# Linear attention, softmax attention and routed experts on 8 cores: token buffer cleared during attention, sums inverted by GpSimd, and the output stage and the end reordered

## The reference

```
xn = layernorm(x)
# recurrent layer, 8 heads of 128
q, k, v = xn Wq^T, xn Wk^T, xn Wv^T
s = (rmsnorm(causal_linear_attention(q, k, v) / denom)) Wo^T
# attention and experts
h1   = rmsnorm(xn) * g1
q    = h1 Wq ;  c = h1 Wdkv ;  k, v = c Wuk, c Wuv        # 16 heads of 64
att  = softmax(causal(q k^T / 8)) v
h2   = xn + att Wo
t    = rmsnorm(h2) * g2
top2 = top_k(t gate_w, 2) ; gates = softmax(top2)           # 8 experts
moe  = sum over the 2 chosen experts e of gate_e * silu(t w1_e) w2_e     # w1: 1024x2048
g    = silu(h2 + moe)
y    = x + s * g
```

## Time and profile before

| what | value |
|---|---|
| time, median of 3 runs | 1753.93 us (1749.98 to 1757.81) |
| the profiled execution | 1748.96 us, its span 1747.4 us |
| spans of the 8 cores | 1722.2 to 1747.4 us, slowest core 6 |
| TensorE matmul busy | 1384.2 us, 79% |
| TensorE weight load busy | 616.0 us, 35% |
| VectorE busy | 724.8 us, 41% |
| ScalarE busy | 583.4 us, 33% |
| GpSimd busy | 387.1 us, 22% |
| moved by DMA | 225.31 MB, mean 129 GB/s |

### The profile page before, as it was taken

How to read it: one execution, slowest core, us unless ns; L and a number is a source line. 1 busy time by engine, 2 the same in 40 slices (tenths; PEclk the granted TensorE clock), 3 DMA queues, 4 the chain that set the end, 5 groups by cost and what they waited for, 6 DMA issues and landing times.

```text
span 1747.4 us, 24421 instructions; the slowest of 8 cores (1722.2 to 1747.4 us)
## 1 busy us (share of the span) xinstructions
PE 1384.2 (79%) x7553; PEld 616.0 (35%) x7665; DVE 724.8 (41%) x1205; ACT 583.4 (33%) x736; POOL 387.1 (22%) x457
## 2 busy tenths in 40 slices
PE   0758899999867788888467319999999999995456
PEld 0324445544312222222133204554555554542122
DVE  2347766548556654433536511212221222123255
ACT  1112222212346688999223202222222222222011
POOL 4212322248442211111103420000000000036410
PEclk9979999999958898999789759999999999998678
DMA  9734435400194000000198679996999997746899
GB/s 203 152 81 114 76 60 96 78 22 1 31 237 154 1 1 1 1 1 1 30 211 216 171 152 186 181 195 127 189 203 185 191 193 142 153 152 211 249 256 253
DMA packets 143427, 225.31 MB, mean 129 GB/s; under 512 B 74160, under 2 KB 81712, under 8 KB 143280
## 3 DMA queue, kind: packets, MB, share of 16 engines
q0 software_dynamic: 51568, 132.91, 39.5%
q1 hardware_dynamic: 91712, 90.43, 19.6%
HBM read 227.14 MB, written 62.45 MB: 166 GB/s over the span
## 4 chain that ended last, share of the span: by engine, by line
PE 57%; DMA 11%; DVE 11%; issue 8%; SPq 6%; ACT 4%; POOL 2%; DVEq 0%; another core or an unknown queue 0%; ACTq 0%; POOLq 0%; PEldq 0%
PE ps L1405 13%; PE pA L1373 7%; PE pB L1373 6%; PE pA L211 4%; PE pA L261 4%; DMA p4a<-ybuf,rcpos 4%; PE ps L790 4%; SPq L1539 3%; ACT ap L805 3%; PE pA L754 3%; PE pB L754 2%; PE pA L215 2%; DMA oxn<-x 2%; PE pw L790 2%; DVE ap L825 2%
## 5 line engine op out<-in xcount | busy, mean ns | idle before, releaser
L1405 PE MATMUL ps<-p3w,mhT 128*128 128x512 bf16 x1116 | 254.3, 381 | 3.8 <-issue 1.9
L805 ACT ACTIVATE ap<-pA,p2nmub 128x1024 bf16<-128x1024 f32 (+1 forms) x160 | 176.2, 1102 | 61.4 <-PE pA L754 56.3
L1528 DVE TENSOR_SCALAR my<-ps,mgate 128x512 f32<-128x512 f32 x78 | 58.3, 750 | 314.2 <-PE ps L1405 311.2
L211 PE MATMUL pA<-fxT,fw 128*128 128x512 bf16 x492 | 127.8, 413 | 67.4 <-DMA fxT<-fxb 41.8
L1405 PEld LDWEIGHTS ps<-p3w,mhT 128*128 128x128 bf16 x1152 | 111.6, 98 | 130.7 <-issue 4.3
L790 PE MATMUL ps<-ap,p2vaug 128*68 128x512 bf16 (+1 forms) x320 | 123.2, 385 | 39.6 <-DVE ap L825 38.5
L805 ACT ACTIVATE ap<-pB,p2nmub 128x1024 bf16<-128x1024 f32 (+3 forms) x160 | 142.2, 889 | 22.6 <-PE pB L754 22.3
L1489 ACT ACTIVATE mh<-pA 128x512 bf16<-128x512 f32 x78 | 46.2, 597 | 307.7 <-PE pA L1373 296.3
L1373 PE MATMUL pA<-p3w,mxT 128*128 128x512 bf16 x576 | 132.7, 384 | 4.7 <-issue 4.7
L1373 PE MATMUL pB<-p3w,mxT 128*128 128x512 bf16 x557 | 126.2, 379 | 1.2 <-issue 0.2
L211 PEld LDWEIGHTS pA<-fxT,fw 128*128 128x128 bf16 x512 | 51.3, 104 | 132.4 <-issue 88.7
(11 more groups left out here) (235 smaller groups left out, 2229.4 us busy)
## 6 DMA issues: line engine op xcount, KB each, us to landing
p3w<-w POOLq DMA_DIRECT2D x16, 4096.0 KB, 37.7
ybuf<-my SPq DMA_DIRECT2D x36, 512.0 KB, 8.0
ybuf<-zero POOLq DMA_DIRECT2D x1, 11776.0 KB, 71.4
mx<-hbuf SPq DMA_DIRECT2D x36, 257.5 KB, 8.2
fx<-x SPq DMA_DIRECT2D x16, 512.0 KB, 5.3
oxn<-x SPq DMA_DIRECT2D x16, 512.0 KB
...
```

The lines of the kernel that those rows point to most:

```text
L211: m = t.matmul(bank, wv[:, n // 8, k, 128 * m0:128 * (m0 + 1)], xv[:, k, :], start=(k == 0), stop=(k == DK - 1))
L805: a.activation(dst[:, :, 0:w], src[:, :, 0:w], AF.Exp, bias=c.p2nmub[:, p % 8:p % 8 + 1]).then_inc(c.a_exp, 1)
L1405: m = t.matmul(c.ps(4 + sl), c.mhT[:, 128 * k:128 * (k + 1)], c.p3w2[:, o:o + 512], start=(k == 0), stop=(k == 15))
L1528: v.tensor_scalar_mul(c.my[n % 2][:, sl * 512:(sl + 1) * 512], c.ps(4 + sl), c.mgate[n % 2][:, :]).then_inc(c.m_yev, 1)
```

## The change

1. *The inverses.* `invert` and its calls leave VectorE. In `att_gpsimd`, POOL raises the four sums to the power of -1 (a constant `minus`, broadcast over 4x1024) straight into the bf16 buffer `arl`, behind the last sum of every fourth unit. TensorE waits for one such instruction a group instead of two.
2. *Clearing.* `clear_results` also clears all of `hbuf`, eight DMAs of 17 x 128 rows from POOL. The eight DMAs at the end of routing, their table `tabzero` and its two VectorE instructions go. POOL waits for the clearing ahead of its first scatter instead of SP ahead of its first load.
3. *o2.* A new `att_sync` on SP turns the 16 tiles of o2 during attention, through one buffer `turn`, into a second DRAM buffer `o2T_sp`; `p4_sync` loads from it without a transpose.
4. *Output stage.* Four buffers `oxn` that lie in the half of `p3w1` that the second expert's weight takes later; SP loads them behind the last product of attention, before the outputs are scaled. TensorE waits for the gate weights only where it uses them first. `ossq` has two buffers. `oh3b` has twelve tiles and scatters go tile by tile from i = 8 on. The first weight comes in four DMAs of 1 MB as written, at i = 2, 5, 8 and 11.
5. *Experts and end.* The four loads of h2 go from POOL to SP, at the start of the last expert, found by a new table `tablast`. SP no longer waits for the results of unused slots. The first expert's first product is issued without a branch. `p4_vector` waits for the lower sum tile by tile instead of for all 16.

The diff, cut:

```diff
 
-    def invert(g):
-
-        l, rl = c.al[g % 2], c.arl[g % 2]
-        v.wait_ge(c.a_ladd, 8 * (g + 1))
-        v.reciprocal(l[64:68, :], l[64:68, :]).then_inc(c.a_rl, 1)
-        v.wait_ge(c.a_rl, 2 * g + 1)
-        if g >= 2:
-            v.wait_ge(c.a_bc, 8 * (g - 1))
-        v.tensor_copy(rl[64:68, :], l[64:68, :]).then_inc(c.a_rl, 1)
...
@@ -842,18 +833,13 @@
             scale(p - 8)
         mask(p, 2)
         mask(p, 3)
-        if p >= 4 and p % 4 == 0:
-            invert(p // 4 - 1)
         v.wait_ge(c.a_pv, FIRST[p + 1])
         if blk:
             v.wait_ge(c.a_ladd, 2 * (p - 7))
         for o, bank in zip((c.aoa, c.aob), o_banks(c, p)):
             v.tensor_copy(o[0:68, 512 * m:512 * (m + 1)],
                           bank[0:68, 0:512]).then_inc(c.a_ev, 1)
-    for p in range(NPAIR - 8, NPAIR - 4):
-        scale(p)
-    invert(7)
-    for p in range(NPAIR - 4, NPAIR):
...
         [128, 2 * (NSLOT - 16), DM // 2])).then_inc(c.y_clear, 16)
+    tokens = c.D["hbuf"].ap().rearrange("(e p r d) -> e p r d", p=128, r=REGION // 128, d=ROW * 2)
+    for e in range(NEXP):
+        g.dma_start(tokens[e], c.zero[:, :].bitcast(U8).unsqueeze(1).broadcast_to(
+            [128, REGION // 128, ROW * 2])).then_inc(c.z_out, 16)
+
+
+def att_sync(s, c):
+
+    for q in range(2):
+        s.wait_ge(c.f_o2out[q], 16 * 8)
+    for i in range(NTI):
+        if i:
+            s.wait_ge(c.t_out, 16 * i)
+        s.dma_start_transpose(c.turn[:, :].rearrange("p (k t) -> p k t", t=128),
+                              tok(c.D["o2_sp"], i)).then_inc(c.t_in, 16)
+        s.wait_ge(c.t_in, 16 * (i + 1))
+        s.dma_start(tok(c.D["o2T_sp"], i), c.turn[:, :]).then_inc(c.t_out, 16)
+    s.wait_ge(c.t_out, 16 * NTI)
 
...
+        if m % 4 == 3:
+            n = p // 4
+            g.wait_ge(c.a_ladd, 2 * (p + 1))
+            if n >= 2:
+                g.wait_ge(c.a_bc, 8 * (n - 1))
+            g.tensor_tensor(c.arl[n % 2][64:68, :], l[64:68, :],
+                            c.minus[64:68, 0:1].broadcast_to([4, 1024]), OP.pow).then_inc(c.a_rl, 1)
...
-TD = 14
+OXN = 4
...
 def o_sync(s, c):
-    s.wait_ge(c.a_mul, 2 * NPAIR)
-    for i in range(NTI + 1):
-        if i < NTI:
-            if i >= 2:
-                s.wait_ge(c.o_h2, 2 * (i - 1))
-            s.dma_start(c.oxn[i % 2][:, :], tok(c.D["x"], i)).then_inc(c.o_xnr[i % 2], 16)
-        if i >= 1:
-            s.wait_ge(c.o_h2, 2 * i)
-            s.dma_start(tok(c.D["h2_sp"], i - 1),
-                        c.oh2[(i - 1) % 3][:, :]).then_inc(c.o_h2out[(i - 1) % 3], 16)
+    s.wait_ge(c.a_pv, len(STEPS))
+    for i in range(OXN):
+        load_rest_x(s, c, i)
+    for i in range(NTI):
+        s.wait_ge(c.o_h2, 2 * (i + 1))
+        s.dma_start(tok(c.D["h2_sp"], i), c.oh2[i % 3][:, :]).then_inc(c.o_h2out[i % 3], 16)
+        if i + OXN < NTI:
+            load_rest_x(s, c, i + OXN)
...
+
+def load_rest_x(s, c, i):
+    s.dma_start(c.oxn[i % OXN][:, :], tok(c.D["x"], i)).then_inc(c.o_xnr[i % OXN], 16)
...
-    t.wait_ge(c.o_gld, 16)
     for i in range(NTI + 4):
...
+            if j == 0:
+                t.wait_ge(c.o_gld, 16)
...
-            if j >= 8:
-                v.wait_ge(c.o_scat[2 * (j % 4)], 16 * (j // 4 - 1))
-                v.wait_ge(c.o_scat[2 * (j % 4) + 1], 16 * (j // 4 - 1))
-            v.scalar_tensor_tensor(c.oh3b[:, ROW * (j % 8):ROW * (j % 8) + DM], c.oh2[j % 3][:, :], c.or3[:, j:j + 1],
+            if j >= 12:
+                v.wait_ge(c.o_scat[2 * (j % 4)], 16)
+                v.wait_ge(c.o_scat[2 * (j % 4) + 1], 16)
+            v.scalar_tensor_tensor(c.oh3b[:, ROW * (j % 12):ROW * (j % 12) + DM], c.oh2[j % 3][:, :], c.or3[:, j:j + 1],
                                    c.g2b[:, :], OP.mult, OP.mult).then_inc(c.o_h3, 1)
...
-
-    v.tensor_tensor(c.rzero[:, :], c.ps(5, 0, 8), c.rcon[:, 32:40], OP.add).then_inc(c.r_zero, 1)
-    v.wait_ge(c.r_zero, 1)
-    v.tensor_scalar_mul(c.tabzero[:, :], c.rzero[:, :], 2.0 * ROW).then_inc(c.r_zero, 1)
...
-    load_w1(g, c, 0)
-    for i in range(NTI + 5):
+    for i in range(NTI + 8):
...
-        if i >= 8 and i % 4 == 0:
-            b = (i - 8) // 4
-            g.wait_ge(c.r_pos, 2 * (b + 1))
-            for q in range(4):
-                j = 4 * b + q
-                g.wait_ge(c.o_h3, j + 1)
-                for k in range(2):
-                    if b:
-                        g.wait_ge(c.o_scat[2 * q + k], 16 * b)
-                    g.indirect_dma_start(
-                        hb, bass.IndirectOffsetOnAxis(c.rpos[:, 16 * k + j:16 * k + j + 1], 0),
-                        c.oh3b[:, ROW * (j % 8):ROW * (j % 8 + 1)].bitcast(U8), None).then_inc(c.o_scat[2 * q + k], 16)
+        if i in (2, 5, 8, 11):
+            load_first_w1(g, c, i // 3)
+        if i == 8:
+            g.wait_ge(c.z_out, 16 * NEXP)
+        if i >= 8:
+            scatter(g, c, hb, i - 8)
+
+
+def scatter(g, c, hb, j):
+
+    g.wait_ge(c.r_pos, 2 * (j // 4 + 1))
+    g.wait_ge(c.o_h3, j + 1)
+    for k in range(2):
+        s = c.o_scat[2 * (j % 4) + k]
+        if j >= 4:
+            g.wait_ge(s, 16 * (j // 4))
+        g.indirect_dma_start(
+            hb, bass.IndirectOffsetOnAxis(c.rpos[:, 16 * k + j:16 * k + j + 1], 0),
+            c.oh3b[:, ROW * (j % 12):ROW * (j % 12 + 1)].bitcast(U8), None).then_inc(s, 16)
+
+
+def load_first_w1(g, c, q):
+
+    g.dma_start(c.p3w1[:, 2 * q * EXPD:2 * (q + 1) * EXPD].rearrange("p (k n) -> p k n", n=EXPD),
+                rows3(c.D["w1_0"])[:, 2 * q:2 * (q + 1), :]).then_inc(c.w1ld[0], 16)
 
 
...
     g.wait_ge(c.ydone, NEXP - 1)
     g.wait_ge(c.r_fin, 10)
     for i in range(NTI + 1):
         if i < NTI:
             if i >= 2:
                 g.wait_ge(c.p4_low, i - 1)
-            if i % 4 == 0:
-                part = c.p4hh[i // 8][:, 4096 * (i // 4 % 2):4096 * (i // 4 % 2 + 1)]
-                g.dma_start(part.rearrange("p (i n) -> p i n", n=DM),
-                            h2[:, i:i + 4, :]).then_inc(c.p4_hld[i // 4], 16)
             gather_result(g, c, c.p4a[i % 2], i, c.p4_ald[i % 2])
         j = i - 1
         if j >= 0:
...
-        load(n)
-    s.wait_ge(c.y_clear, 16)
-    for n in range(NSLOT):
-        if n + MXN < NSLOT:
...
-        s.wait_ge(c.m_yev, 2 * (n + 1))
-        if n < SURE:
-            store(n)
-        else:
...
+    def load_rest():
+
+        h2 = c.D["h2_sp"].ap().rearrange("(i p) n -> p i n", p=128)
+        for q in range(4):
+            s.dma_start(c.p4hh[q // 2][:, 4096 * (q % 2):4096 * (q % 2 + 1)].rearrange(
+                "p (i n) -> p i n", n=DM), h2[:, 4 * q:4 * q + 4, :]).then_inc(c.p4_hld[q], 16)
+
...
+                    if n + 1 >= NEXP - 1:
+                        with s.register(f"rest{n}") as q:
+                            s.reg_load(q, c.tablast[0:1, n + 1:n + 2])
+                            with s.If_ne(q, 0):
+                                load_rest()
...
+        with s.register(f"out{n}") as r:
+            s.reg_load(r, c.tabval[0:1, n:n + 1])
+            with s.If_ne(r, 0):
+                s.wait_ge(c.m_yev, 2 * (n + 1))
+                store(n)
+                hand_on(n)
+            with s.Else():
+                s.wait_ge(c.m_yst[n % 2], 16 * (n // 2))
+                s.sem_inc(c.m_yst[n % 2], 16)
...
-    new_w1(0)
-    up(0, 0)
-    up(0, 1)
+
+    t.wait_ge(c.w1new, 1)
+    t.sem_inc(c.w1new, -1)
+    t.wait_ge(c.m_xev, 1)
+    up_with(0, 0, 0)
+    up_with(0, 1, 0)
...
+        s.dma_start(c.p4o[q][:, :], tok(c.D["o2T_sp"], i)).then_inc(c.p4_in[q], 16)
         s.dma_start(c.p4x[q][:, :], tok(c.D["x"], i)).then_inc(c.p4_in[q], 16)
 
...
 def p4_vector(v, c):
-    v.wait_ge(c.p4_low, NTI)
     for i in range(NTI + 1):
         if i < NTI:
...
-        ("tabnew", 40, I32, 0), ("tabval", 40, I32, 0), ("tabodd", 40, I32, 0), ("tabzero", 8, I32, 0), ("rzero", 8, F32, 0)])
-    region(route, [("oxn", DM, F32, 2), ("oh2", DM, F32, 3), ("oh3b", 8 * ROW, BF16, 0),
+        ("tabnew", 40, I32, 0), ("tabval", 40, I32, 0), ("tabodd", 40, I32, 0)])
+    c.tablast = c.rcmp[:, 0:40].bitcast(I32)
+    region(w1_end - DK * EXPD * 2, [("oxn", DM, F32, OXN)])
+    region(route, [("oh2", DM, F32, 3), ("oh3b", 12 * ROW, BF16, 0),
```

More of the change, by code:

```diff
@@ L852, in att_vector @@
                           bank[0:68, 0:512]).then_inc(c.a_ev, 1)
-    for p in range(NPAIR - 8, NPAIR - 4):
-        scale(p)
-    invert(7)
-    for p in range(NPAIR - 4, NPAIR):
+    for p in range(NPAIR - 8, NPAIR):
         scale(p)
@@ L1268, in p3_sync @@
     hb = c.D["hbuf"].ap()
-    s.wait_ge(c.z_set, 1)
-    s.wait_ge(c.r_zero, 2)
-    for e in range(NEXP):
-        with s.register(f"zero{e}") as r:
-            s.reg_load(r, c.tabzero[0:1, e:e + 1])
-            row = s.snap(r, donate=True, min_val=0, max_val=(HROWS - 128) * ROW * 2)
-            s.dma_start(hb[bass.ds(row, 128 * ROW * 2)].rearrange("(p n) -> p n", p=128),
-                        c.zero[:, :].bitcast(U8)).then_inc(c.z_out, 16)
-    s.wait_ge(c.r_tab, 18)
```

(48 more changed lines are left out.)

47 lines of the change are left out of this document (26 added, 21 removed).

## The result

| | before | changed |
|---|---|---|
| time, median | 1755.87 us (4 runs) | 2997.0 us (2990.56 to 2999.36, 4 runs) |
| ratio to before | | 1.708, 95% interval 1.702 to 1.714 |
| profiled execution, span | 1747.4 us (core 6) | 2993.2 us (core 1) |

The account below looks back on a forecast made before the run. No engine fills the span, so the chain of waits, read by stage, was taken as the bound. Terms -2 -5 -12 -5 -27 -15 -13 = -79 from 1749, plus 5, gave 1675 us, range 1620 to 1755.

Parts of the forecast that it names:

- point 1: Attention: inverses as powers on POOL, 7 us each; gains of 2 us in the middle and 5 us at the end.
- Rival A: Attention: each power is slow, 157 us along the line of short powers; time about 2870 us, chance 0.19.
- Point 2: Clearing moved into attention costs 0; scatters at the end of routing land without zeros beside them, gaining 12 us.
- Rival D: Attention: issuing the clear holds POOL to 555 or 660 us; time 1705 to 1775 us, chance 0.08.
- Point 3: Attention: sixteen transposes of o2 on SP, done by about 465 us, at cost 0.
- Point 4: Output stage: shorter gate weight wait gains 5 us; the loop falls to 95 us, gaining 27 us.
- Rival B: Output loop and end: DMA rates of 228 and 249 GB/s are the limit; time 1730 us, chance 0.17.
- Point 5: End: h2 loads moved to SP shorten the lower gathers by 15 us; the last stretch gains 13 us.
- the last stretch: End, the last 103 us: without transpose issue on SP it takes 90 us, gaining 13 us.
- the 7 us of the inverses: Attention: the gains of 2 us in the middle and 5 us at the end from inverses on POOL.

Follow-up runs that it names:

- power_shapes: The kernel before with eight POOL instructions, mostly powers of different shapes, behind its last work and VectorE copies and products beside them; the 4x1024 power took 163.4 us.
- powers_alone: The kernel before with only the eight inverses turned into powers on POOL; 2776.6 us, ratio 1.581.
- clear_by_sp: The changed kernel with the inverses back on VectorE and the eight clearing transfers issued by SP instead of POOL; 1691.2 us, ratio 0.965.
- clear_late: The changed kernel with the inverses back on VectorE and the token buffer cleared by SP behind the routing, as before; 1719.0 us, ratio 0.978.
- h2_by_pool: clear_by_sp with the four loads of h2 back on POOL between the lower gathers; 1700.1 us, ratio 0.971.
- transposes_late: clear_by_sp with the 16 transposes of o2 back in the last stage on SP; 1709.3 us, ratio 0.974.

## Why the prediction was wrong

The time, 2997 us, lies outside the range of 1620 to 1755, and on the other side: slower, which had a chance of 0.20. The step that failed is in point 1, "Between ends so far apart I take 7 us, what VectorE's reciprocal of the same 4x1024 takes", with its reason that the powers of up to eight elements "are mostly start and fill". The two rows at hand gave 153 ns an element, and power_shapes measured 160 all the way to 1024. The line through them ended at 157 us, the power takes 163.2. The reason leaned on a row of another engine and another operation against two rows of the same engine and the same operation. It also read its own slope wrongly: a start and fill would have shown in the first element, 595 ns, and it did; the 153 of each further one were what was left without them.

Rival A had the mechanism: the power is slow and every group waits for it. Its 2870 us are near the result for a wrong reason. It added 8 times 150 us to attention as it was. But attention's own work runs inside the links, so that 8 links of 172 us take the place of its time instead of adding to it: powers_alone shows 1011 us more, and by the prediction's own sum A should have been near 2690. Another 298 us are the hold of POOL, by which the first power of the changed kernel starts at 798.8 instead of 500.8 us. Less 9 us between the last power and the first output matmul (powers_alone stands 8.3 us there for its gate weights), that makes the 1300.

The masks were to stand as long as a power, for which the prediction named the Trainium skill's rule that the loser waits for the whole instruction (SBUF — State Buffer, section Who interferes with whom). They stood for half of it, 81.8 of 163.2 us, and products beside powers of 512 elements not at all; here the measurement decides. (The page has those words for VectorE's two-port modes, which a copy can take, and the copy did stand for the whole power of 4x1024, 163.28 us. Beside one of 512 elements it did not.) The pace was POOL's own, sums behind powers: behind a mask that stood until 1225 POOL was still in its power until 1306, so masks added nothing to it.

Point 2, clearing: "Cost 0, covered by a DMA that now moves 1 GB/s there" failed as well. The cover was right for the transfers (clear_by_sp moves them in attention for nothing), not for the engine that issues them. Rival D named it, with 555 to 660 us for POOL's release, from 310 and 165 GB/s, and 1705 to 1775 us. POOL was released at 789 us, while the zeros drained at 129 GB/s with the DMA engines full, and the hold by itself costs 312 us. A and D were priced as alternatives; they came together.

Of point 2's gain, 12 us by scatters that land without zeros beside them, 17.6 were measured between clear_late and clear_by_sp (57.8 against 40.2), but only 7 against the kernel before (46.8).

Point 3, transposes at no cost on SP, held: they ended at about 450 us, and nothing waited for them.

Point 4: the gate wait went. The loop was forecast at 95 us and took 101.3 to 109.3 in the six kernels with the change's order and no zeros beside it; by the end that the prediction used (994.0 before) it is some 4 us less. Its bytes bound it as forecast: 23.8 MB in clear_by_sp and clear_late, at 230 and 218 GB/s. The bytes were put a little low (23.1) and the rate too high (243). The Trainium skill's rule that the prediction drew on (DMA: Bandwidth & Descriptors, section Issuing engines are not separate DMA queues) is borne out by the trace: 4.2 MB less on POOL's queue made the loop shorter by 13 us, though POOL's and SP's loads are issued apart. Rival B had the rate right, 228 GB/s, but not what it drew from it, that the loop would gain nothing: 27 us were forecast, 16 to 24 gained.

Point 5: 15 us for h2, where h2_by_pool shows 9. 13 us for the last stretch, where the changed kernel shows 14 and transposes_late 16 to 18.

The other terms of the sum, all but the 7 us of the inverses, come to -72; clear_by_sp, which has all parts but the powers and the issue by POOL, is 59 us below the kernel before (1750.6 us in its comparison). At 1691.2 us it beats both kernels.
